# A message-passing layer on one core: 12 instead of 16 node rows per loop body picked by matmul, and the masked messages in a tile of their own

## What is computed

```python
m_in = concatenate([x[src], x[dst], edge_attr], axis=-1)   # 400000 x 144
h = silu(m_in @ W1 + b1)                                   # 400000 x 64
messages = silu(h @ W2 + b2)
agg = segment_sum(messages, dst, num_segments=12500)
upd = silu(concatenate([x, agg], axis=-1) @ W3 + b3)
out = layernorm(x + upd)                                   # over the 64 features
```

## Time and profile before

| | before |
|---|---|
| median of 3 executions | 3622.36 us (3621.96 to 3623.26) |
| profiled execution, its own time | 3622.36 us |
| its span, first to last instruction | 3620.5 us |
| mean granted TensorE clock | 0.946 of full speed |
| busy: TensorE matmul / VectorE / ScalarE / GpSimd | 3134.8 / 2755.5 / 1083.0 / 2713.9 us |

### The profile page before, as it was taken

One profiled execution on the slowest core, in us unless ns is written; L12 is line 12 of the kernel. 1 busy time (PEld: TensorE's weight loads), 2 busy tenths in 40 slices (PEclk: granted clock), 3 DMA queues, 4 the chain that ended last, 5 costly groups with the idle time before them and its releaser, 6 DMA issues.

```text
span 3620.5 us, 55874 instructions
## 1 busy us (share of the span) xinstructions
PE 3134.8 (87%) x16900; PEld 2260.4 (62%) x16900; DVE 2755.5 (76%) x6365; ACT 1083.0 (30%) x1687; POOL 2713.9 (75%) x2879
## 2 busy tenths in 40 slices
PE   4898889888888988888898888988988898888985
PEld 2666666666666666666666666666656666665663
DVE  7787777877777787777778777777777777777785
ACT  1232322323233232323333232332323233232232
POOL 7777777777777777777777777777777777777775
PEclk9899999999999999999999999999999999999997
DMA  7111111121112112111211111121111211111111
GB/s 172 36 35 40 41 42 35 38 46 37 40 35 49 35 37 47 37 40 35 48 35 37 40 42 42 35 45 39 37 40 35 49 35 37 40 42 42 34 31 28
DMA packets 326718, 152.87 MB, mean 42 GB/s; under 512 B 214558, under 2 KB 280127, under 8 KB 326422
## 3 DMA queue, kind: packets, MB, share of 16 engines
q0 software_dynamic: 91808, 94.20, 11.8%
q1 hardware_dynamic: 232774, 54.48, 7.2%
q10 hardware_dynamic: 1840, 0.34, 0.1%
HBM read 139.17 MB, written 9.62 MB: 41 GB/s over the span
## 4 chain that ended last, share of the span: by engine, by line
PE 40%; DVE 28%; POOL 17%; issue 12%; DMA 2%; DVEq 0%; POOLq 0%; ACT 0%; ACTq 0%; SPq 0%
PE pick_ps L1084 24%; POOL edge_in L488 17%; PE z_ps L1046 6%; DVE rows_T L813 5%; DVE z_ps L778 4%; DVE pair L782 4%; DVE every L774 3%; PE in_ps L1022 3%; PE z_ps L1040 3%; PE agg_ps L1059 2%; DVE kept L826 2%; DVE edge_in L749 2%; DMA edge_in<-in_x_dram,src_i 1%; DVE pair L785 1%; PE pick_ps L1069 1%
## 5 line engine op out<-in xcount | busy, mean ns | idle before, releaser
L488 POOL DMA_INDIRECT edge_in<-in_x_dram,src_i x2869 | 2712.7, 946 | 876.1 <-issue 862.2
L1084 PE MATMUL pick_ps<-parts,rows_T 128*128 128x512 f32 (+1 forms) x6656 | 1876.5, 418 | 0.0
L1084 PEld LDWEIGHTS pick_ps<-parts,rows_T 128*128 128x128 f32 x6656 | 1170.3, 198 | 536.2 <-issue 311.6
L576 ACT ACTIVATE z_ps<-z_ps,zero_col 128x512 f32<-128x512 f32 x391 | 258.9, 662 | 1261.0 <-DVE z_ps L763 1261.0
L568 ACT COPY in_T<-in_ps 128x1024 f32<-128x1024 f32 x391 | 396.2, 1013 | 755.9 <-PE in_ps L1022 735.4
L1022 PE MATMUL in_ps<-ident,edge_in 128*128 128x128 f32 x3128 | 421.9, 278 | 148.9 <-DMA edge_in<-in_x_dram,src_i 113.6
L1022 PEld LDWEIGHTS in_ps<-ident,edge_in 128*128 128x128 f32 x3128 | 365.8, 143 | 233.3 <-issue 163.3
L1046 PEld LDWEIGHTS z_ps<-w_bd,h_T 128*128 128x128 f32 x3128 | 459.7, 216 | 28.9
L1046 PE MATMUL z_ps<-w_bd,h_T 128*128 128x128 f32 x3128 | 469.3, 299 | 0.0
L763 DVE TENSOR_TENSOR z_ps<-z_ps,b_rep 128x512 f32<-128x512 f32 x391 | 272.1, 696 | 222.9 <-PE z_ps L1046 221.1
L813 DVE TENSOR_TENSOR rows_T<-pick_ps,key_of 128x896 fp32r<-128x896 f32 x257 | 280.5, 1091 | 207.5 <-PE pick_ps L1069 203.5
(11 more groups left out here) (101 smaller groups left out, 1778.3 us busy)
## 6 DMA issues: line engine op xcount, KB each, us to landing
edge_in<-in_x_dram,src_i POOLq DMA_INDIRECT x2869, 2.4
ea<-in_edge_attr_dram SPq DMA_DIRECT2D x48, 512.0 KB, 4.4
w_in<-node_terms SPq DMA_DIRECT2D x391, 12.0 KB
node_terms<-h_T SPq DMA_DIRECT2D x12, 256.0 KB
node_terms<-lot_T SPq DMA_DIRECT2D x12, 256.0 KB, 2.4
y<-in_x_dram SPq DMA_DIRECT2D x15, 192.0 KB, 4.4
term<-node_terms SPq DMA_DIRECT2D x15, 192.0 KB
out_dram<-y SPq DMA_DIRECT2D x15, 192.0 KB, 2.3
```

Source lines behind the costliest of these rows:

```text
L488: pool.indirect_dma_start(out=edge_in[:, to_slot, t, XS], out_offset=None, in_=x[:, :], in_offset=bass.IndirectOffsetOnAxis(ap=indices[:, ...
L1084: last = nc.tensor.matmul(pick_ps[r][:, 0:(b - a) * H], rows_T[:, i % 2, c, :], parts[:, j, a:b, :].rearrange("p k f -> p (k f)"), start=( ...
```

## The change

`PER_BODY` goes from 16 to 12: 12 picked tiles for each body instead of 16, in every second group instead of two groups in three. All places of the picks' pieces follow from it. The product with the mask no longer overwrites `z2_ps`: it goes to a new SBUF tile `masked`, and the second sum reads that tile. VectorE's wait for the first sum moves behind the wait for the second. One wait of TensorE before the first piece of a pick's second round is gone.

```diff
-    PER_BODY = 16
+    PER_BODY = 12
...
+        masked = sb("masked", [P, C])
...
                 nc.vector.tensor_reduce(every[:, :], z2_ps[:, :].rearrange("p (k f) -> p f k", f=H),
                                         AX.X, ALU.add).then_inc(s_every, 1)
-                dve.wait_ge(s_every, done(k, v))
-                messages = z2_ps[:, :].rearrange("p (c a f) -> p c a f", a=2, f=H)
-                nc.vector.tensor_mul(messages, messages,
+                nc.vector.tensor_mul(masked[:, :].rearrange("p (c a f) -> p c a f", a=2, f=H),
+                                     z2_ps[:, :].rearrange("p (c a f) -> p c a f", a=2, f=H),
                                      beyond[...]).then_inc(s_masked, 1)
                 dve.wait_ge(s_masked, done(k, v))
-                nc.vector.tensor_reduce(pair[:, v % 2, 1, :], z2_ps[:, :].rearrange("p (k f) -> p f k", f=H),
+                nc.vector.tensor_reduce(pair[:, v % 2, 1, :], masked[:, :].rearrange("p (k f) -> p f k", f=H),
                                         AX.X, ALU.add).then_inc(s_other, 1)
+                dve.wait_ge(s_every, done(k, v))
                 dve.wait_ge(s_other, done(k, v))
                 nc.vector.tensor_sub(pair[:, v % 2, 0, :], every[:, :], pair[:, v % 2, 1, :]).then_inc(s_pair, 1)
...
                     pe.wait_ge(s_rowsT, n + 1)
-                if (r, c) == (1, 0) and not (isinstance(k, int) and n == 0):
-
-                    pe.wait_ge(s_picked, n * ROUNDS)
```

## The result

The changed kernel takes 3708.5 us (3707.32 to 3710.17, four runs) against 3622.56 us: ratio 1.0238, 95% interval 1.0220 to 1.0255. The forecast was 3703 us, with a range from 3699 to 3711. The profiled execution took 3709.15 us, its span is 3707.2 us.

The account below looks back on a forecast made before the run. The prediction took GpSimd's gathers, end to end at 1.248 us each, as the bound: span 3620.5 + 79.9 (64 more gathers) + 0.9 (tail) = 3701.3 us, plus 1.9 gives 3703 us; range 3699 to 3711.

Parts of the forecast that it names:

- Gathers end to end: GpSimd never pauses, so 64 more gathers at 1.248 us each add 79.9 us to the path; chance 0.91.
- The tail: After the last gather, three passes with the slower second sum, 0.3 us each, add 0.9 us.
- The masked tile costs nothing here: VectorE's product and second sum through SBUF: net about +0.3 us a group, 117 us, beside the gathers.
- TensorE's wait costs nothing: Removing TensorE's wait before round two neither costs nor gains; its matmuls had 0.0 us of idle time before them.
- The loop's own pace at 12 picks: Loop of TensorE and VectorE goes from 8.90 to about 8.0 us a group; waits for gathers begin near 550 us.
- The picks' term: In the loop's pace: fewer pick matmuls take 1.2 us a group off TensorE.
- The masked tile's term: In the loop's pace: VectorE's slower second sum out of SBUF, net about +0.3 us a group.
- Rival 1: Loop of TensorE and VectorE becomes the bound, at 9.28 us a group: 3755 us; chance 0.04.
- Rival 2: VectorE's second sum out of SBUF stops GpSimd's gathers, 418 us more, about 4120 us; chance 0.01.
- Rival 3: TensorE sets the pace and the gathers' gap is a wait for its slots: 352 us less, 3270; chance 0.02.
- Rival 4: GpSimd's time is one for each group, however many gathers, so no change: 3623 us; chance 0.02.

Follow-up runs that it names:

- e3: Changed kernel with 63 gathers left out, all other engines' work kept: 3629.95 us, ratio 1.0016.
- e7: Kernel before with TensorE's new order of e6 and 18 picked tiles for each body instead of 16: 3582.51 us, ratio 0.9886.
- e1: Kernel before with only the picks cut from 16 to 12 for each body; mask in PSUM and TensorE's wait stay: 3705.77 us, ratio 1.0227.
- e2: Kernel before with only the masked tile in SBUF, 16 picks and TensorE's wait kept: 3656.87 us, ratio 1.0100.
- e4: Changed kernel with TensorE's wait before the first piece of round two put back: 3709.24 us, ratio 1.0238.
- e6: Kernel before with the picks' pieces of a group's first place put ahead of the previous group's window sum on TensorE: 3625.20 us, ratio 1.0002.
- e5: e2 with the product written so that the second sum reads SBUF with unit stride: 3696.78 us, ratio 1.0207.
- e10: Kernel before with 18 picked tiles for each body, TensorE's order unchanged, on another chip: 4774.92 us, ratio 1.0111 to the kernel before there.
- e11: Changed kernel with the second sum made twice in every group, on another chip: 4745.30 us, ratio 1.0043 to the kernel before there.

## Why the prediction was right, and where its terms were off

*Gathers end to end.* Right, and shown: e3 gives 1.25 us for each gather left out, and e7 and e1, with 32 fewer and 64 more in their picks' place, give 1.31 and 1.29 us each. The term was 79.9 us and measured 83.1. The price of a regular gather held (481 in 600 us). The 3.2 us are longer gathers: 26 starts before, and some 40 after, stand more than 1.27 us from the next, together 5.1 and 8.3 us over 1.248 each. In the changed kernel many of them return every 180 gathers, which is what one body of the loop issues: near the 300th, 660th, 840th, 1020th, 1560th, 1740th and so on. What lengthens them wasn't tried.

*The tail.* The term was 0.9 us and measured 3.7. Each pass was priced at 0.3 us and took 0.25: the sum is 0.33 us longer (0.376 in the working), and the product begins 0.61 us after the first sum instead of 0.72, since the wait is gone. But only two of the three passes lie on the path behind the last gather: 0.5 us. The clock gave 1.0 us, which the range held as a possible 3. The 2.1 us ahead of the update weren't foreseen. All profiles with 12 picks have them, e1 without the masked tile, and what TensorE waits for there isn't known.

Together the two terms miss 6 us of span, 3707.2 against 3701.3; the median is 5.5 us above the forecast. That it still fell inside the range is the merit of the few us allowed for the clock and for slow gathers, and in part luck, as a third of the miss has a cause that the range didn't name.

*The masked tile costs nothing here.* Right for this change: e1 and the changed kernel differ by under 3 us. The working priced it at 117 us of VectorE, hidden as long as the loop stays under the gathers' pace. The sum lay on the loop in full, 0.3 us a group (6.71 in e1, 7.02 in the changed kernel), and only the cover hid it. e2 shows what it costs when that cover is thin: at 16 picks, the extra 0.19 us a group keep the loop from making up for its late start, and the time rises by 34 us. A pace under the gathers' isn't enough, then; the prediction's condition was too mild. The two parts of the change, alone, cost 34 and 83 us; together they cost 86. They don't add, since the longer of two paths counts.

*TensorE's wait costs nothing.* Right (e4). The working says that the last read of `pick_ps1` comes some groups earlier; by the code it is 4 of the 72 places, one and a third groups, and a wait for a later pair lies between. At 16 picks it is 2 or 3 places, and for every second pick no such wait lies between. By the code, the matmuls into `pick_ps1` would there no longer be ordered behind VectorE's last read; such a kernel wasn't tried.

*The loop's own pace at 12 picks.* Mis-sized. The sum took 1.2 us a group off for TensorE, put 0.3 on and came to 8.0; TensorE's waits for gathers were to begin near 550 us. They began between 300 and 350. The step that failed is the pace of the loop, in two of its terms. The picks' term was 1.2 us, TensorE's matmuls alone; e1 shows 1.8 (8.50 against 6.71). That VectorE's share of a pick makes the difference is likely, but no run separates it. And the start was 8.90, a mean over later bodies, while groups 6 to 24 of the kernel before took 8.50; in that stretch no lot of nodes is finished yet. Whether the lots are the 0.4 us wasn't tried. The masked tile's term, 0.3, held. With 7.02 us a group, TensorE reaches group 30 near 308 us, where its waits begin. It doesn't touch the time, since it only widens a margin.

*The rivals.* Rival 1 (the loop becomes the bound) didn't come about in the changed kernel; it is what e2 shows at 16 picks. Its formula, start plus 391 times the pace plus tail, overstates: 98 + 391 x 9.09 + 28 = 3680 us, against a span of 3645.3. The first body took 8.61 us a group, and the seven groups without picks at the end about 6.1. Rival 2 (SBUF sums hold GpSimd up) is out by the gathers' unchanged length in the changed kernel. Rival 3 (TensorE sets the pace) is out by e1 and e6: a loop that was faster by 1.8 and by 0.8 us a group gained nothing. Rival 4 (a price for each group) is out by e3: fewer gathers in the same groups gave all.

The Trainium skill (SBUF — State Buffer, "Door 1: The DMA port swizzle") says that each access which crosses to a new 16-byte line of SBUF pays a penalty; it gives no figure for VectorE. e5 agrees in both directions: the strided sum took 1034 ns in e2 and 686 with unit stride, and the product written with a stride went from 680 to 1098 ns.

## What to carry to other kernels

When an engine never stops, count its instructions and the time between two starts. That product is the floor, whatever its busy share says; here it was 75% busy and the bound. The cost of an edit beside it depends on the margin of the second-slowest loop, so find that loop's own pace in a stretch where it has not yet caught up, before calling anything hidden. The margin isn't the difference of the two paces alone: a loop that starts late must also make up for its start, as e2 shows. A gain for the second loop is worth nothing by itself, but it can be spent: e6 gained nothing, and e7, with two more picks in a body, came out 1.1% faster by moving work off the bound. That e7 needed the new order isn't shown, since the run with 18 picks and the old order, e10, was on the other chip.

## What the hardware showed unexpectedly

An indirect gather of 64 rows took 1.20 us from start to start, one of 128 rows 1.25 us. Writing SBUF with a 32-byte stride from a PSUM source slowed a 128x512 product from 680 to 1098 ns, about as much as reading with a 256-byte stride slowed the sum (686 to 1034 ns), while the same stride in PSUM cost nothing visible (691 ns). And another chip ran the same kernel before in 4720.71 us instead of 3622, with waits of up to 13 us without a named releaser. There, 12 picks with one sum too many (e11) were 0.4% longer than the kernel before, where 12 picks on the first chip were 2.3 to 2.4% longer: a ranking found on one chip need not hold there.
